# A bidirectional GRU in 1024 steps: fills dealt out one per gap, and the rest of each gap given to matmuls whose result nobody reads

## The reference

```python
xn = (x - mu) / jnp.sqrt(var + 1e-05) * ln_gamma + ln_beta       # x: 16 images, 32 x 32, 128 channels
...                                                              # a small MLP picks a scan order (idx) per image
seq = jnp.where((idx == 1)[:, None, None], seq_v, seq_h)         # [16, 1024, 128]
z = seq @ in_w.T + in_b
yf = _gru_dir(z @ gru_wih_f.T + gru_bih_f, gru_whh_f, gru_bhh_f, False)
yb = _gru_dir(z @ gru_wih_b.T + gru_bih_b, gru_whh_b, gru_bhh_b, True)
y = jnp.concatenate([yf, yb], axis=-1) @ out_w.T + out_b
return x + y.reshape(Bx, Hx, Wx, C)
...
def step(h, xt):                                                 # _gru_dir scans this over 1024 tokens
    gh = h @ whh.T + bhh
    xr, xz, xn = jnp.split(xt, 3, axis=-1)
    hr, hz, hn = jnp.split(gh, 3, axis=-1)
    r = jax.nn.sigmoid(xr + hr)
    z = jax.nn.sigmoid(xz + hz)
    n = jnp.tanh(xn + r * hn)
    h_new = (1.0 - z) * n + z * h
```

## Time and profile before

| | |
|---|---|
| median of 3 runs | 1904.64 us (1901.84 to 1905.37) |
| the profiled execution | 1902.69 us, of which the span is 1900.9 |
| TensorE busy over the span | 1639.2 us (86%), 21315 matmuls |
| VectorE busy | 1602.0 us (84%), 9056 instructions |
| ScalarE busy | 1226.8 us (65%), 6271 instructions |
| GpSimd busy | 58.1 us (3%), all of it before the recurrence |
| memory traffic over the span | 14 GB/s |
| f16 matmuls of 16 columns | 18432, mean 182 ns |
| f32 input fills, passes of 128 columns | 1536, mean 491 ns |
| state scans | 2048, mean 292 ns |

### The profile page before, as it was taken

How to read it: one execution, slowest core, us unless ns; L and a number is a source line. 1 busy time by engine, 2 the same in 40 slices (tenths; PEclk the granted TensorE clock), 3 DMA queues, 4 the chain that set the end, 5 groups by cost and what they waited for, 6 DMA issues and landing times.

```text
span 1900.9 us, 65131 instructions
## 1 busy us (share of the span) xinstructions
PE 1639.2 (86%) x21315; PEld 1248.0 (66%) x21315; DVE 1602.0 (84%) x9056; ACT 1226.8 (65%) x6271; POOL 58.1 (3%) x131
## 2 busy tenths in 40 slices
PE   3558989898989989898998999898988999898987
PEld 2336666666666666666666666666666666666665
DVE  7788888888888888888888888888888888888887
ACT  7935666666666666666666666666666666666665
POOL 4420000000000000000000000000000000000000
PEclk9655555555555555555555555555555555555555
DMA  4200000000000000000000000000000000000000
GB/s 152 67 7 10 11 13 11 13 10 14 11 12 12 11 13 11 14 10 13 11 13 5 12 12 12 12 12 12 10 13 11 12 12 12 12 12 12 10 13 13
DMA packets 40133, 31.27 MB, mean 16 GB/s; under 512 B 3449, under 2 KB 37625, under 8 KB 39801
## 3 DMA queue, kind: packets, MB, share of 16 engines
q1 hardware_dynamic: 39800, 27.13, 4.9%
HBM read 18.73 MB, written 8.39 MB: 14 GB/s over the span
## 4 chain that ended last, share of the span: by engine, by line
PE 68%; DVE 16%; ACT 9%; issue 6%; DMA 0%; DVEq 0%; POOL 0%; SPq 0%; ACTq 0%; POOLq 0%
PE bank L592 67%; DVE bank L875 5%; DVE state L887 4%; ACT rec L496 3%; ACT rpair L490 3%; DVE halves L896 3%; DVE big L866 1%; ACT big L432 1%; ACT zquad L493 1%; DVE rec L902 1%; ACT seq L428 1%; DMA gamma_row<-in_gamma 0%; DVE stats L721 0%; DVE seq L850 0%; DVEq L886 0%
## 5 line engine op out<-in xcount | busy, mean ns | idle before, releaser
L592 PEld LDWEIGHTS bank<-halves,wsplit 128*128 128x128 f16 x18432 | 726.7, 107 | 535.1 <-DVE halves L896 386.7
L592 PE MATMUL bank<-halves,wsplit 128*128 128x16 f16 x18432 | 876.9, 182 | 187.2 <-DVE halves L896 185.1
L887 DVE TENSOR_TENSOR_SCAN state<-zquad,rec 128x64 f32<-128x64 f32 x2048 | 597.2, 292 | 180.4 <-ACT rec L496 134.2
L490 ACT ACTIVATE rpair<-bank 128x16 f32<-128x16 f32 x2048 | 380.5, 186 | 337.7 <-PE bank L592 319.7
L592 PE MATMUL bank<-seq,wcomb 128*128 128x128 f32 x1536 | 593.0, 491 | 0.4 <-DVE seq L850 0.4
L496 ACT ACTIVATE rec<-bank 128x16 f32<-128x16 f32 x2048 | 406.3, 198 | 284.1 <-DVE bank L875 82.3
L875 DVE TENSOR_TENSOR_SCAN bank<-rpair,bank 128x32 f32<-128x32 f32 x2048 | 445.6, 218 | 49.4 <-ACT rpair L490 25.0
L896 DVE SCALAR_TENSOR_TENSOR halves<-state 128x32 f16<-128x32 f32 x2048 | 430.6, 210 | 34.8
L493 ACT ACTIVATE zquad<-bank 128x16 f32<-128x16 f32 x2048 | 406.7, 199 | 19.8
L592 PEld LDWEIGHTS bank<-seq,wcomb 128*128 128x128 f32 x1536 | 385.9, 312 | 1.3 <-DVE seq L850 1.3
L902 DVE TENSOR_TENSOR rec<-state,signs 128x32 f32<-128x32 f32 x2047 | 372.8, 182 | 3.1
(11 more groups left out here) (118 smaller groups left out, 203.5 us busy)
## 6 DMA issues: line engine op xcount, KB each, us to landing
xin<-in_x SPq DMA_DIRECT2D x16, 512.0 KB, 3.7
big<-in_x SPq DMA_DIRECT2D x128, 64.0 KB
out<-big SPq DMA_DIRECT2D x128, 64.0 KB
wih<-in_wiht SPq DMA_DIRECT2D x2, 384.0 KB
con<-in_consts SPq DMA_DIRECT2D x1, 424.0 KB, 5.2
whh<-in_whht SPq DMA_DIRECT2D x2, 192.0 KB
inw<-in_in_w SPq DMA_DIRECT2D x1, 128.0 KB
outw<-in_outwt SPq DMA_DIRECT2D x2, 64.0 KB
```

The lines of the kernel that those rows point to most:

```text
L490: act.activation(rpair[:, e, 2 * B * d:2 * B * (d + 1)].rearrange("p (n k) -> p n k", k=2)[:, :, 1], R[q][:, at:at + B], ACT.Sigmoid, scal ...
L592: return nc.tensor.matmul(o, w, m, start=start, stop=True, skip_group_check=True)
L887: v.tensor_tensor_scan(state[:, d, ring, :], zquad[:, e, cols], rec[:, e, cols], 0.0, ALU.mult, ALU.add).then_inc(state_ready[d], 1)
```

## The change

It is made in TensorE's stream, and for the two additions in VectorE's. The gate biases move from s = 1 to 4 to s = 0 to 3, the input fills from s = 1 to 6 to s = 2 to 7. The projection of direction 0 moves from between the directions to behind direction 1 at s = 0, that of direction 1 to behind direction 1 at s = 1, and the output bias between the directions at s = 4, where it raises `y_ready`. VectorE's additions move from s = 3 and 5 to s = 5 and 7. A new function `spin` issues f16 matmuls of 128 columns, 128 x 128 weights of their own, into columns 256 to 383 of the other half's bank R, which nothing reads: between the directions one at s = 0, 1 and 4, none at s = 2 and 3, three at s = 5, 6 and 7, and one behind direction 1 at every s.

```diff
-        FILL_BIAS = [None, G_R, G_Z, G_HN, G_N, None, None, None]
-        FILL_INPUT = [None, (G_R, 0), (G_Z, 0), (G_R, 1), (G_N, 0), (G_Z, 1), (G_N, 1), None]
+        FILL_BIAS = [G_R, G_Z, G_HN, G_N, None, None, None, None]
+        FILL_INPUT = [None, None, (G_R, 0), (G_Z, 0), (G_R, 1), (G_N, 0), (G_Z, 1), (G_N, 1)]
+        SPIN = [P, P, 0, 0, P, 3 * P, 3 * P, 3 * P]
+
+        def spin(q, n):
+
+            for at in range(0, n, P):
+                mm(R[q][:, 2 * P:3 * P], wsplit[:, 0, 0, 0:HID], wsplit[:, 0, 1, at:at + P])
+
...
         def output_bias():
-            mm(Y[:, 0:C], ones3[:, :], obias[:, :])
+            return mm(Y[:, 0:C], ones3[:, :], obias[:, :])
...
                 step(base, r, 0)
+                if filling and FILL_BIAS[s] is not None:
+                    fill_bias(1 - q, FILL_BIAS[s])
+                if s == 4 and done >= 0:
+                    output_bias().then_inc(y_ready, 1)
+                if filling:
+                    spin(1 - q, SPIN[s])
+                step(base, r, 1)
                 if s == 0 and done >= 0:
                     if done > 0:
                         pe.wait_ge(y_used, 2 * done)
                     project(1 - q, 0)
-                if filling and FILL_BIAS[s] is not None:
-                    fill_bias(1 - q, FILL_BIAS[s])
-                step(base, r, 1)
-                if s == 0 and done >= 0:
-                    output_bias()
-                    project(1 - q, 1).then_inc(y_ready, 1)
+                if s == 1 and done >= 0:
+                    project(1 - q, 1)
                 if filling and FILL_INPUT[s] is not None:
                     fill_input(1 - q, kblk + (q + 1), *FILL_INPUT[s])
+                if filling:
+                    spin(1 - q, P)
...
         project(1, 0)
-        output_bias()
-        project(1, 1).then_inc(y_ready, 1)
+        project(1, 1)
+        output_bias().then_inc(y_ready, 1)
...
-                if s in (3, 5) and kblk + q > 0:
-                    add_output(kblk + q - 1, s // 4)
+                if s in (5, 7) and kblk + q > 0:
+                    add_output(kblk + q - 1, (s - 5) // 2)
```

## The result

The changed kernel took 1919.13 us in the median of 4 runs (1917.39 to 1922.35), against 1904.72 for the kernel before; the ratio is 1.0081 with a 95% interval of 1.0062 to 1.0099. The clock did not rise in the loop. Of the cases weighed it is B, the one on the slower side, whose sum was 1924 us; the forecast, A, was wrong.

What follows compares the result with a forecast made beforehand. An undisturbed step was taken as a 1.617 us chain of latencies, TensorE owning 0.29. At 2.4 GHz a block falls from 13.77 to 12.72 us, 132 us over 126 blocks: 1902.69 to 1770 us, range 1745 to 1935.

Steps and rivals of the forecast that it cites:

- B: Slower rival: clock stays at 1.2 GHz and spins push the steps, mainly in the long gap; 1924 us, chance 0.25.
- A: Forecast case: the clock rises to 2.4 GHz in the loop's first blocks and stays; 1770 us, chance 0.60.
- part 3 of the change: What the spins on TensorE can do to the clock: filling the gaps was to bring 2.4 GHz; it decides the sum.
- 0.36 of the 0.44 us in a short gap: Between the directions, nine small matmuls leave 0.44 us free; three spins, or a bias and one spin, fill 0.36.
- Rival C: Clock in the loop rises and falls again and again, half the blocks fast, half slow; 1847 us, chance 0.08.
- TensorE's 0.29: From direction 0's nine small matmuls to its reset sigmoid: TensorE's 0.29 us of the step's 1.617 us latency chain.
- The term of 0.045 a step: Small matmuls in the step's chain at 2.4 GHz: lower latency shortens each step by 45 ns, bounds 0 and 65.
- the 0.29 us of the strided biases: Two candidate biases with strided output overfill short gaps, costing 0.29 us a block; gone at 2.4 GHz only.
- The dealing out: Each projection gets its own long gap; output bias, fills, gate biases and additions move; gains 0.45 us a block.
- rival D: Spins neither raise the clock nor cost anything, only the moved work counts: 51 us less at most (1852), chance 0.07.
- The 0.45 of the projections: Both projections, with the output bias, overfill one step's gaps by some 0.45 us a block; moving them removes it.
- The additions: VectorE's two output additions, moved to steps 5 and 7, lengthen their steps by 0.045 us each, 0.09 a block.

Runs made afterwards that it cites:

- burst_after: The changed kernel with 48 more f16 matmuls of 256 columns between step 16 and step 17; 1926.05 us, ratio 1.0131 to the kernel before.
- heavy: The changed kernel with about twice the spins in matmul work, 69 matmuls of 128 columns a block; 1865.0 us, ratio 0.981 to the kernel before.
- deal_r1: deal_only with four matmuls instead of three for the reset gate, the last issued twice; 1864.6 us, ratio 0.9792 to the kernel before.
- warm1: heavy with fewer spins where its steps were stretched, 56 a block, and 10 per long gap in the first 16 steps; 1975.3 us, ratio 1.0389.
- deal_only: The changed kernel without its 2,540 spin matmuls, everything else where the change puts it; 1847.6 us, ratio 0.9718 to the kernel before.
- deal_halves: deal_only with each of the two strided candidate biases cut into two matmuls of 128 columns; 1809.2 us, ratio 0.9501 to the kernel before.

## Why the prediction was wrong, point by point

**The clock (part 3 of the change, case A at 0.60): wrong, and the step that failed.** The prediction let the clock rise in the first blocks because the spins fill the gaps; it stayed at 0.50 over the 1700 us read, with 2,540 spins in the loop, and without the rise every term of the gain at 2.4 GHz falls away. I saw rightly that busy records don't tell whether the clock will rise, and then went by a count of the same kind: 0.36 of the 0.44 us in a short gap filled. Nothing in the rows said that this would do, and the row that spoke against it (3.04 of 3.40 us busy, no rise) I gave too little weight. The runs show 69 spins a block raising and holding the clock, 20 neither raising it nor holding it behind a burst, and the numbers between alternating. Rival C's objection, that a stretch with 2.38 us busy of 3.40 kept the clock, was also read for more than it was worth: burst_after shows it falling with no idle record at all. Why `heavy` holds the clock and the others don't stays open.

**What the clock would bring: wrong, and independent of the first.** Even where it was granted, the forecast's 1770 was out of reach. Here the failed step is that TensorE's 0.29 is in a ring that bounds the step, so that a faster matmul shortens it: a chain of starts that follow each other closely isn't the only such chain. "Every link starts as soon as the one before it has ended" was read too kindly: the sigmoid ends at 513.88 and the candidate starts at 513.94, a wait that deal_r1 halves (505.43 and 505.46) without a longer step. VectorE runs both directions in one order, and its ring with ScalarE takes the same 1.62 us. I had seen half of it (the candidate of direction 1 right behind the state scan of direction 0), and did not follow it round. The term of 0.045 a step measured nothing: the small matmul went from 182 to 173 ns in the mean (heavy's group has 173), matmul to sigmoid from 285 to 270, the step stayed at 1.62. The estimate from the Trainium skill ("TensorE: Matmul & The Clock Gate", Part 2, "Single matmul latency") was 23 ns, for a matmul alone. The 9 ns of the records and the 15 to the sigmoid, in a stream where matmuls overlap, lie below it. For the undisturbed steps the upper clock brings nothing; what it could bring here was the 0.29 us of the strided biases, as warm1's stretches show, 36 us in all, and that came cheaper by cutting them in two.

**The dealing out: right.** 1852 forecast for rival D's upper end, 1847.6 measured. The 0.45 of the projections went.

**The additions: wrong, in the sum only 0.09 a block.** The step of 1.66 that I put down to VectorE's addition is the one behind the stretched steps; deal_only has it without an addition in it, and deal_halves has none of it with both additions in the open.

**The spins at the lower clock, case B: right in the main place; the sum, 1924 for 1919, is in part luck.** The long gap is where they press most. Of its terms the last four steps were 1.677 for 1.67, the strided ones 1.88 for 1.83 and 1.84, the first two 1.667 for 1.76. These two are the mis-sized term: I had the nine matmuls take 0.23 and a bias with a spin 0.36, but the bias starts 0.37 behind the first of the nine (504.86, 505.23), the spin 0.32 behind the bias (505.55) and the next nine 0.08 behind the spin, so the short gap was 0.77 (504.86 to 505.63) for 0.67. In the kernel before the same 0.32 stands between the bias at 505.37 and the next nine, but ended nearly in time. The 0.19 a block that this adds is met by 0.10 too much for the strided steps, 0.09 for additions that cost nothing, and less in the last four: the errors cancel to 5 us.

## What to carry to other kernels

Before paying for a faster engine, follow every ring that closes in the step time, above all the one through an engine that serves two interleaved streams in a fixed order; if two rings are about equally long, speeding up a piece of one buys nothing. Price a piece by adding a little to it and by taking a little from the other ring: two such runs settled here what a page of timeline had left open. And where an instruction doesn't fit a gap, cut the instruction before filling the others.

## What the runs showed of the hardware

The granted clock did not follow TensorE's busy records: 0.50 over 1700 us with 1698.65 busy (the changed kernel), 1.00 over 1600 us with 1595.42 busy (`heavy`), and the two kernels differ in their spins alone, 20 a block against 69. It fell some 4 us behind a burst although no idle record followed (`burst_after`). A matmul of 16 columns gained 9 ns of 182 in its mean record from twice the clock, and 15 ns from its start to the sigmoid that reads its sum. At the lower clock a strided bias of 128 columns lasts 0.39 us (`deal_halves`, 505.68), as long as a contiguous one of 256 (505.23 in the changed kernel), and a strided one of 256 lasts 0.60 (508.75); at the upper clock that one lasts 0.38 (`warm1`, 442.01).
